# Filler products ahead of the last group's scores and in the tail, and two projections moved ahead of feed-forward products, in a one-core macaron block

## The reference: what is computed

```python
x = x + 0.5 * ffn(layernorm(x))
x = x + attn(layernorm(x))          # 16 heads of 16, rotary positions, causal softmax, projection
x = x + 0.5 * ffn(layernorm(x))     # the same weights again

def ffn(x):                          # xp is x shifted by one token
    xr = mu_r * x + (1 - mu_r) * xp
    xk = mu_k * x + (1 - mu_k) * xp
    return sigmoid(xr @ W_r.T) * (square(relu(xk @ W_k.T)) @ W_v.T)
```

## Time and profile before

| | |
|---|---|
| median of 3 runs | 3127.63 us (3127.12 to 3133.78) |
| the profiled execution's own time | 3128.23 us |
| its span, first to last instruction | 3126.5 us |
| mean granted TensorE clock | 0.986 of full |
| TensorE busy | 2973.8 us (95%) |
| VectorE busy | 2511.6 us (80%) |
| ScalarE busy | 2159.5 us (69%) |
| GpSimd busy | 1566.1 us (50%) |

### The profile page before, as it was taken

How to read it: one execution, slowest core, us unless ns; L and a number is a source line. 1 busy time by engine, 2 the same in 40 slices (tenths; PEclk the granted TensorE clock), 3 DMA queues, 4 the chain that set the end, 5 groups by cost and what they waited for, 6 DMA issues and landing times.

```text
span 3126.5 us, 57247 instructions
## 1 busy us (share of the span) xinstructions
PE 2973.8 (95%) x18245; PEld 1667.7 (53%) x18245; DVE 2511.6 (80%) x8326; ACT 2159.5 (69%) x4802; POOL 1566.1 (50%) x2190
## 2 busy tenths in 40 slices
PE   6899999999999999999999999999999999999987
PEld 5444555555555555555555555555555555555434
DVE  3888888888888888888888888888888888888862
ACT  4476677776777777777776777777777676777664
POOL 5455455555454455555555455455555555454322
PEclk8899999999999999999999999999999999999998
DMA  3443243443334253343343334243343433343411
GB/s 99 78 86 65 63 98 68 85 88 75 83 76 91 64 100 73 69 97 68 85 88 74 83 77 92 64 100 74 69 96 69 83 88 75 83 76 79 78 45 38
DMA packets 202593, 245.56 MB, mean 79 GB/s; under 512 B 68405, under 2 KB 104245, under 8 KB 202293
## 3 DMA queue, kind: packets, MB, share of 16 engines
q1 hardware_dynamic: 202293, 241.90, 37.3%
HBM read 53.48 MB, written 51.38 MB: 34 GB/s over the span
## 4 chain that ended last, share of the span: by engine, by line
PE 69%; DVE 15%; ACT 7%; issue 4%; POOL 3%; DMA 1%; SPq 1%; POOLq 0%; DVEq 0%; ACTq 0%
PE ps_y L720 15%; PE ps_s L689 13%; PE ps_m L699 11%; DVE ps_m L926 7%; PE ps_d L779 7%; PE ps_d L773 6%; PE ps_d L785 5%; PE ps_d L776 5%; ACT pt_sb L815 4%; PE ps_d L766 3%; PE ps_d L727 2%; PE ps_d L789 2%; DVE dif_sb L956 1%; DVE ka_sb L950 1%; DVE sw_sb L979 1%
## 5 line engine op out<-in xcount | busy, mean ns | idle before, releaser
L815 ACT ACTIVATE pt_sb<-ps_s 128x512 f32<-128x512 f32 (+3 forms) x3072 | 1464.8, 494 | 839.8 <-PE ps_s L689 829.7
L926 DVE CUSTOM_DVE_ANT_0 ps_m<-ps_m,mask_sb 128x512 f32<-128x512 f32 (+3 forms) x3072 | 1676.1, 570 | 446.9 <-PE ps_m L699 429.7
L689 PE MATMUL ps_s<-qr_sb,kr_sb 99*128 99x512 bf16 (+3 forms) x3072 | 1008.2, 331 | 55.1 <-ACT pt_sb L815 42.7
L699 PE MATMUL ps_m<-kr_sb,qr_sb 96*128 96x512 bf16 (+3 forms) x3072 | 1000.5, 329 | 42.6 <-DVE mx_sb L926 38.0
L1057 POOL TENSOR_SCALAR_AFFINE_SELECT pt_sb<-pt_sb 128x512 f32<-128x512 f32 x512 | 330.7, 646 | 845.1 <-ACT pt_sb L815 844.1
L720 PE MATMUL ps_y<-pt_sb,v_sb 128*32 128x512 f32 (+3 forms) x6144 | 593.4, 496 | 1.2 <-POOL pt_sb L1057 1.2
L689 PEld LDWEIGHTS ps_s<-qr_sb,kr_sb 99*128 99x128 bf16 x3072 | 294.8, 96 | 527.2 <-issue 233.8
L699 PEld LDWEIGHTS ps_m<-kr_sb,qr_sb 96*128 96x128 bf16 x3072 | 302.0, 98 | 325.9 <-DVE mx_sb L926 96.9
L926 DVE DVE_READ_ACCUMULATOR2_ANT mx_sb<- 128x1 f32 x3072 | 431.6, 140 | 0.0
L785 PE MATMUL ps_d<-axn_sb,wqk_sb 128*128 128x256 f32 x1024 | 306.1, 397 | 4.0 <-ACT axn_sb L857 3.9
L773 PE MATMUL ps_d<-ka_sb,wk_sb 128*128 128x256 f32 x1024 | 305.6, 395 | 1.0 <-DVE ka_sb L950 0.9
(11 more groups left out here) (92 smaller groups left out, 3273.7 us busy)
## 6 DMA issues: line engine op xcount, KB each, us to landing
kr_sb<-part_sb SPq DMA_DIRECT2D x378, 128.0 KB, 4.4
qr_sb<-part_sb SPq DMA_DIRECT2D x378, 128.0 KB, 4.7
y_way<-yt_sb SPq DMA_DIRECT2D x128, 256.0 KB, 2.7
sw_sb<-qb_sb SPq DMA_DIRECT2D x496, 64.0 KB, 2.0
x_sb<-x SPq DMA_DIRECT2D x64, 256.0 KB, 2.8
yn_sb<-y_way SPq DMA_DIRECT2D x64, 256.0 KB
den_sb<-r_way SPq DMA_DIRECT2D x64, 256.0 KB
out<-x_sb SPq DMA_DIRECT2D x64, 256.0 KB, 2.2
```

The lines of the kernel that those rows point to most:

```text
L689: eng.matmul(ps_s[:, slot % NS, 0:width], kr_sb[0:KR + NP, n % RS, j, kb * P:(kb + 1) * P], qr_sb[0:KR + NP, n % RS, j, q0:q0 + width], st ...
L699: eng.matmul(ps_m[:, u % NM, 0:width], qr_sb[0:KR, n % RS, j, i * P:(i + 1) * P], kr_sb[0:KR, n % RS, j, piece * QC:piece * QC + width], s ...
L815: eng.activation(pt_sb[:, buffer, j, column:column + width], ps_s[:, slot % NS, 0:width], ACT.Exp, scale=SCALE).then_inc(exped, 1)
L926: eng.tensor_tensor_reduce(ps_m[:, u % NM, 0:width], ps_m[:, u % NM, 0:width], mask_sb[:, m0:m0 + width], 1.0, -3e38, ALU.add, ALU.max, mx ...
```

## The change

A function `keep_going` issues products of 256 columns in float32, 128 x 128 weights from `wk_sb`, into the last buffer of `ps_m`. Nobody reads them. They wait, the first time, until all maxima are taken.

- One stands ahead of each score from slot 3016 on: 56 of them, 8 at the end of the last group but one and 48 in the last.
- In the tail, four follow the transposes of chunks 124 and 126, two those of 125 and 127, and six the last projection: 18.
- The planner's numbers change: the second feed-forward of the first half of the last batch has its lags halved, the statistics come one slot sooner after the projection, and `p_P` 62 and 63 are due earlier.

```diff
@@ Plan.describe @@
-            came = ("xp", i, 2) if second else ("load", i, 8 if b else 0)
+            came = ("xp", i, 1 if b == nb - 1 else 2) if second else ("load", i, 8 if b else 0)
+            near = (lambda lag: math.ceil(lag * 0.5)) if second and b == nb - 1 and c < NCH // 2 else (lambda lag: lag)
...
-            s("POOL", "f_rstd", p, 1.3, t, ("f_st1", p, 3), ("f_x1", p - 2, 1))
-            s("ACT", "f_x0", p, 0.36, t, ("f_rstd", p, 4))
+            s("POOL", "f_rstd", p, 1.3, t, ("f_st1", p, near(3)), ("f_x1", p - 2, 1))
+            s("ACT", "f_x0", p, 0.36, t, ("f_rstd", p, near(4)))
...
-                t = (b + 1) * BSLOTS - 16 + 8 * c + 12 * (c // 2)
-                s("PE", "p_P", i, 4, t, ("y_mul", NQC * (b * NP2 + NP2 - 1) + c // 2, 3))
+                last = b == nb - 1 and c >= NCH // 2
+                t = nb * BSLOTS - 40 + 2 * c if last else (b + 1) * BSLOTS - 16 + 8 * c + 12 * (c // 2)
+                s("PE", "p_P", i, 4, t, ("y_mul", NQC * (b * NP2 + NP2 - 1) + c // 2, 1 if last else 3))
@@ TensorE @@
+            def keep_going(times):
+
+                pe.wait_ge(max_taken, n_groups * NU)
+                for _ in range(times):
+                    eng.matmul(ps_m[:, NM - 1, 0:C], wk_sb[:, 0, 0:P], wk_sb[:, 1, :], start=True, stop=True)
+
@@ dense, after the transposes of f_T @@
+                    b, c, second = plan.ffn[i]
+                    if second and b == nb - 1:
+                        keep_going(2 if c % 2 else 4)
@@ dense, after the last matmul of a p_P @@
+                        if i == nb * NCH - 1:
+                            keep_going(6)
@@ the loop over slots @@
                 if slot in SCORE_AT:
+                    if slot >= n_ticks * G - GSLOTS - 8:
+                        keep_going(1)
                     score(SCORE_AT[slot])
```

More of the change, by code:

```diff
@@ L129, in describe @@
             i = b * NCH + c
-            came = ("xp", i, 2) if second else ("load", i, 8 if b else 0)
+            came = ("xp", i, 1 if b == nb - 1 else 2) if second else ("load", i, 8 if b else 0)
+            near = (lambda lag: math.ceil(lag * 0.5)) if second and b == nb - 1 and c < NCH // 2 else (lambda lag: lag)
             s("DVE", "f_st0", p, 0.33, t, came, ("f_st1", p - 1, 0))
             s("DVE", "f_st1", p, 0.51, t, ("f_st0", p, 0), ("f_x1", p - 2, 1))
-            s("POOL", "f_rstd", p, 1.3, t, ("f_st1", p, 3), ("f_x1", p - 2, 1))
-            s("ACT", "f_x0", p, 0.36, t, ("f_rstd", p, 4))
+            s("POOL", "f_rstd", p, 1.3, t, ("f_st1", p, near(3)), ("f_x1", p - 2, 1))
+            s("ACT", "f_x0", p, 0.36, t, ("f_rstd", p, near(4)))
             s("ACT", "f_x1", p, 0.36, t, ("f_x0", p, 0))
-            s("PE", "f_T", p, 0.5, t, ("f_x1", p, 2))
+            s("PE", "f_T", p, 0.5, t, ("f_x1", p, near(2)))
             s("ACT", "f_xn", p, 0.48, t, ("f_T", p, 1), ("f_r1", p - 2, 1), ("f_dif", p - 1, 1))
-            s("POOL", "f_dif", p, 1.2, t, ("f_xn", p, 2), ("f_R", p - 2, 1), ("f_xadd", p - 2, 1))
-            s("DVE", "f_k0", p, 0.62, t, ("f_dif", p, 2), ("f_V", p - 2, 1))
+            s("POOL", "f_dif", p, 1.2, t, ("f_xn", p, near(2)), ("f_R", p - 2, 1), ("f_xadd", p - 2, 1))
+            s("DVE", "f_k0", p, 0.62, t, ("f_dif", p, near(2)), ("f_V", p - 2, 1))
             s("DVE", "f_k1", p, 0.62, t, ("f_k0", p, 0))
@@ L142, in describe @@
             s("DVE", "f_r1", p, 0.46, t, ("f_r0", p, 0))
-            s("PE", "f_K", p, 4, t, ("f_k1", p, 3))
+            s("PE", "f_K", p, 4, t, ("f_k1", p, near(3)))
             s("ACT", "f_relu", p, 0.5, t, ("f_K", p, 1))
             s("ACT", "f_sq", p, 0.55, t, ("f_relu", p, 0))
-            s("PE", "f_R", p, 4, t, ("f_K", p, 0), ("f_r1", p, 3))
+            s("PE", "f_R", p, 4, t, ("f_K", p, 0), ("f_r1", p, near(3)))
             s("ACT", "f_tanh", p, 0.47, t, ("f_R", p, 1))
-            s("PE", "f_V", p, 4, t, ("f_R", p, 0), ("f_sq", p, 2))
-            s("DVE", "f_u", p, 0.61, t, ("f_V", p, 1), ("f_tanh", p, 2))
-            s("POOL", "f_xadd", p, 1.2, t, ("f_u", p, 2))
+            s("PE", "f_V", p, 4, t, ("f_R", p, 0), ("f_sq", p, near(2)))
+            s("DVE", "f_u", p, 0.61, t, ("f_V", p, 1), ("f_tanh", p, near(2)))
+            s("POOL", "f_xadd", p, 1.2, t, ("f_u", p, near(2)))
             if second:
```

## The result

The changed kernel takes **3134.21 us** (median of 10 runs, 3131.29 to 3140.03) against 3125.99 us for the one before (10 runs, 3122.89 to 3133.78): ratio 1.0027, 95% interval 1.0018 to 1.0036. It is slower, by 5.6 to 11.3 us. The forecast was 3130.5 in a range of 3124.5 to 3137.0, with the larger chance on "within 0.2%" and 0.22 on slower by more: the time lies in the range, on the side of the smaller chance, and the loss is about three times the 2.7 us of the sum.

What follows compares the result with a forecast made beforehand. ScalarE paced the last group's loop at full clock, with products TensorE would; 4.7 us lost there less 2.0 won in the tail made 2.7 longer, 3130.9 on the profiled execution, forecast 3130.5 us, range 3124.5 to 3137.0.

Steps and rivals of the forecast that it cites:

- the sum: Whole kernel: 4.7 us lost in the last group, 2.0 won back in the tail, so 2.7 us longer.
- The bound of the loop: Last group: product and wide score take 0.65 us of TensorE, above the exponential's 0.54, so TensorE becomes the bound.
- the pace of wide scores: Last group: scores of 512 columns 0.65 us from start to start, the pace that half clock gave before.
- The sum is 46.4 us ... 4.7 us later: Last group: products, scores, projections and bursts at full clock; last score starts at about 3084.9 instead of 3080.2.
- The tail: From the last score to the end, seven steps at full clock: 2.0 us won back, ending at 3129.2.
- the last `pv` behind the four products: Tail: last `pv` waits for four products (1.73 us), not the select, and starts at 3088.0, 6.4 us later.
- the wait ahead of `p_P` 62: Tail: the moved projections wait 0.9 us for `y_mul` before they run.
- step 6: Tail: 2.6 us of unhidden filler delays the transposes of 126; `f_K` 126 starts at 3113.8 (before 3108.60).
- rival A: Last group: products run free in waits for the exponential, 0.54 us a score; about 3120 us, chance 0.08.
- B: Last group: the clock falls all the same, a product costs 0.87 us; 3140 us, chance 0.10.
- C: Tail: the clock falls, about 1.8 us a fall; 3132.3 us, or 3134 for two; chance 0.17.
- D: Tail: the moved projections become a wait, blocking `f_R` and `f_V` of 125 until `y_mul` 63; 3133 us, chance 0.10.

Runs made afterwards that it cites:

- e8_double: The change with two products of 256 columns ahead of each score instead of one: 3158.93 us (2 runs), ratio 1.0102 to the kernel before.
- e3_no_tail: The change without its 18 products in the tail: 3131.99 us, ratio 1.0015 to the kernel before.
- e7_bf16: The change with all 74 products as bf16 ones (96 rows, 128 x 256 columns): 3121.46 us, ratio 0.9983 to the kernel before.
- e1_planner: The change without any of its 74 products, only the planner's numbers: 3125.08 us, ratio 0.9997 to the kernel before.
- e11_idle_only: e10_idle_spots without the 56 products ahead of the scores: 3120.24 us, ratio 0.9979 to the kernel before.
- e6_only_512: The change with products ahead of the 24 scores of 512 columns alone, none in the tail: 3124.34 us, ratio 0.9988 to the kernel before.
- before_3: The kernel before, unchanged, profiled a third time for the clock of its last group: 3123.57 us (1 run).
- e2_scores: The kernel before with only the 56 products ahead of the scores added: 3133.13 us, ratio 1.0022 to the kernel before.
- e10_idle_spots: The change with bf16 products ahead of the scores and, in the tail, only where TensorE waits: 3119.76 us, ratio 0.9982 to the kernel before.
- e4_narrow: The change with all 74 products of 128 columns instead of 256: 3124.99 us, ratio 0.9995 to the kernel before.

## Why the prediction was right or wrong

**The bound of the loop and the pace of wide scores: right.** TensorE became the bound, wide scores 0.65 us apart. The second product of e8_double cost 24.07 us where the price of the first gave 24.1.

**"The sum is 46.4 us ... 4.7 us later": the term that was mis-sized.** From the first product to the last score it was 49.0 us (3039.81 to 3088.80) instead of 46.4, and the group grew by 7.3 us, not 4.7. I had one price, 0.43 us, from a row between scores of 256 columns, and bursts taken from places without a product behind them. The timeline after shows 0.06 us more behind each of the 11 scores of 128 columns that have a product or a projection behind them (0.7 us), 0.1 more behind each of 8 bursts (0.8) and 0.09 more for the matmul ahead of each burst (0.7). These make 2.2 of the 2.6 us missing. Another 0.2 us is in the products behind wider scores, 0.44 us each behind the 20 of 512 columns and not 0.43, and 0.06 us is a bf16 matmul of 128 columns (L764) that the sum left out.

**The tail: right, step by step, and 0.5 us short in all.** It won 1.5 us, not 2.0. The two normalizations between the last exponentials, the last `pv` behind the four products (3.4 us behind the last score; I had 3.1), `pv` to `y_mul` in 11.65 us (11.7), the wait ahead of `p_P` 62 of 0.74 us (0.9), the six products unhidden (2.6), `f_dif` 126 behind `f_xadd` 125, six products in 10.4 us (3118.18 to 3128.62). From the last score to the end of the span it was 44.8 us (I had 44.3). That the six products undo the moved projections fits e3_no_tail, 2.5 us shorter without the tail's products even with a fall of the clock. It isn't shown by itself: that run leaves out all 18, the four ahead of the last `pv` too, which then starts 2.00 us behind the last score instead of 3.39. Two slips of the working changed little: the terms of step 6 add up to 3113.5 and not 3113.8, and in rival A eight scores at 0.11 us give 0.9 and not 1.1.

**The sum against the median: too small a gap also from the base.** The sum was made on one execution that had 20 us of half clock in the group. Two more profiles had 10, and 1.3 us less in the last stretch. One profile is one draw of it; I took it for the rule. And there was luck in the number: the difference was missed by 5.3 us (8.2 against 2.9), the time by only 3.7, because the median of three runs that the forecast stood on, 3127.63, lay 1.6 us above that of ten.

**Rivals.** A (the product is free) fell: wide scores start 0.65 us apart, and the group grew by 7.3 us. It would be nearly true of another product, the bf16 one of 0.11 us (group of 39.21 us in e7_bf16). B (half clock all the same) fell, nine profiles of nine. The Trainium skill (page "TensorE: Matmul & The Clock Gate", section "Why this matters for your kernels") ties the fall to long idle gaps between bursts. The filled loop agrees with that. The three profiles of the kernel before, e1_planner and e11_idle_only don't: they show 10 to 27 us of half clock in a group without a wait above 0.6 us. C (a fall in the tail) didn't come in the change itself; it did in six of the kernels without its tail products or with smaller ones. D (the moved projections wait) came with 0.74 us, at the size that was in the sum.

**The 131 ns.** The Trainium skill (page "TensorE: Matmul & The Clock Gate", section "Back-to-back issue gap") gives 131 ns for a bf16 matmul of 512 columns in a sustained stream. The trace doesn't agree: with TensorE never idle, a score of 512 columns took 0.22 us (3047.86 to 3048.08), and score and product together 0.65.

**What stays open.** In the fourteen profiles the last stretch begins anywhere from 3030.1 to 3039.8 us, though the code in front of slot 3016 is the same. That is more than the 5.8 to 7.1 us that the change loses in the stretch. It goes with the time at half clock ahead of it, summed in the same way: 31 us in e6_only_512, the first to get there, 34 in before_3 and e2_scores (3033.7 and 3035.0 us), 48 to 58 in the eight that get there after 3038 us. The fit isn't exact (51 us in the profile before, at 3037.05), and why that time differs between executions is open.

Why e11_idle_only has e10's median is answered in part. Its ten executions are the longer the lower their mean granted clock: 3114.34 to 3116.15 us at 0.993 or 0.994, 3129.18 at 0.988, the profiled one. As an estimate from these, a mean of 0.993 is some 44 us at 0.50 in the whole execution; 0.988 is 75 us, of which the profile shows 48 ahead of the last stretch and 27 in the group. So that profile is the extreme of its ten, and how much half clock its usual execution has in the group isn't known.

## What to carry to other kernels

Filler for the clock has a price that its place sets: in a loop of two engines it is free only up to the wait that is there, so take the cheapest product that holds the clock (here bf16 at 0.11 us instead of float32 at 0.43) and put it where TensorE waits, not between a finished input and the instruction that starts a long chain. The last stretch was shortest that way (75.37 us in e10_idle_spots), but the medians of e7_bf16, e10_idle_spots and e11_idle_only, 3119.8 to 3121.5 us, don't tell which of the three placings is best. When a price is taken from one alternation, look at how it changes at narrow neighbours and at the ends of bursts before multiplying it by 56. And when what is to be gained is a clock that falls in one execution and less in the next, take several profiles of the kernel before: one shows a draw, not the gain.

## What the runs showed of the hardware that was not expected

- The granted clock was 1.00 through the last group with bf16 products of 0.11 us (e7_bf16, e10_idle_spots) as with float32 ones of 0.43 us, and with 24 products (e6_only_512) as with 56.
- Half clock came and went between executions of one kernel: about 20, 10 and 10 us of it in the same group in three profiles of the kernel before, in a loop that had no wait above 0.6 us in any of the three. And the ten executions of e11_idle_only are the longer the lower their mean clock: 3114 us at 0.993, 3129 at 0.988.
- A product of 256 columns in float32 holds TensorE 0.43 us behind a score of 512 columns, 0.49 behind one of 128 and 0.54 behind a burst of `pv`, and the score ahead of a burst 0.31 instead of 0.22, at full clock and with nobody waited for.
- Weight loads of 0.19 us, two to a float32 product, did not hold a product of 128 columns at 0.38 us in e4_narrow: it took 0.22 us behind a score of 512 columns and 0.29 behind one of 128.
